# A recommendation tower rewritten: 11 instead of 9 tables by one-hot matmul, split tables kept in an HBM scratch

## The reference

```python
e = stack([tbl_f[ids[:, f]] for f in range(26)], axis=1)      # 2048 x 26 x 128, fp32
combined = concatenate([dense[:, None, :], e], axis=1)        # 27 features of 128 per sample
inter = einsum('bfd,bgd->bfg', combined, combined)            # 27 x 27 per sample
z = concatenate([dense, inter[:, iu, ju]], axis=1)            # 128 + 351 pairs above the diagonal
h = relu(concatenate([z, dense], axis=1) @ W_top1 + b_top1)   # 607 -> 512
h = relu(h @ W_top2 + b_top2)                                 # 512 -> 256
y = h @ W_top3                                                # 256 -> 1
```

## Time and profile before

| | |
|---|---|
| median of three runs | 431.82 us (426.78, 431.82, 437.46) |
| the profiled execution: its span, which is its time here | 432.4 us |
| prologue, to the first gram | 0 to 79 us |
| a block in the loop | 99 us |
| last gather issued | 392.3 us |
| data moved | 49.5 MB, 115 GB/s |

### The profile page before, as it was taken

The page is one execution under the profiler, slowest core; times in us unless marked ns, Lnnn a source line. Parts: engine busy times, 40 slices in busy tenths (PEclk is TensorE's granted clock), DMA queues, the critical chain, the costliest instruction groups (busy, mean ns, idle before and its releaser), DMA issues.

```text
span 432.4 us, 13310 instructions
## 1 busy us (share of the span) xinstructions
PE 330.4 (76%) x5360; PEld 266.8 (62%) x5360; DVE 239.1 (55%) x471; ACT 179.4 (41%) x363; POOL 308.9 (71%) x280
## 2 busy tenths in 40 slices
PE   0785719677699998286879999376969999867596
PEld 0563517466578876275668877264758887656475
DVE  2776625397569563266768664075666758023531
ACT  2144223720746546220546545420564546323442
POOL 6887878887778877777778878777777877772000
PEclk9899977888979999659969999666879999986699
DMA  5467853435435345426444543526354442221000
GB/s 155 153 177 191 239 167 109 128 92 151 115 110 149 118 122 117 133 52 167 119 130 114 158 116 106 141 55 169 77 172 100 142 123 71 55 57 28 5 0 0
DMA packets 24707, 49.51 MB, mean 115 GB/s; under 512 B 8010, under 2 KB 10586, under 8 KB 24653
## 3 DMA queue, kind: packets, MB, share of 16 engines
q1 hardware_dynamic: 15916, 30.83, 22.4%
q0 software_dynamic: 8704, 17.84, 17.5%
q10 hardware_dynamic: 32, 0.01, 0.0%
HBM read 48.65 MB, written 0.01 MB: 113 GB/s over the span
## 4 chain that ended last, share of the span: by engine, by line
PE 65%; issue 15%; DMA 10%; ACT 5%; DVE 3%; SPq 0%; ACTq 0%; DVEq 0%
PE mix_ps L454 12%; PE emb_ps L436 12%; PE emb_ps L438 11%; PE emb_ps L416 6%; DMA lookup_ids<-ids_looked_up 5%; DMA table<-table 5%; PE mlp_ps L485 4%; PE mlp_ps L488 4%; PE mlp_ps L486 4%; PE mlp_ps L436 3%; PE mlp_ps L438 3%; DVE one_hot L650 2%; ACT emb L535 2%; PE mlp_ps L498 2%; PE mlp_ps L501 2%
## 5 line engine op out<-in xcount | busy, mean ns | idle before, releaser
L396 POOL DMA_INDIRECT rows<-table,gather_ids x272 | 307.9, 1132 | 83.6 <-issue 81.7
L650 DVE TENSOR_SCALAR one_hot<-lookup_ids,row_number 125x512 fp32r<-125x512 int32 x288 | 124.8, 490 | 43.6 <-DMA lookup_ids<-ids_looked_up 17.6
L436 PE MATMUL emb_ps<-one_hot,table_h 125*128 125x512 f32 x224 | 94.2, 421 | 19.1 <-DVE table_l L640 18.7
L454 PE MATMUL mix_ps<-emb 128*26 128x26 f32 x4096 | 57.7, 202 | 54.3 <-issue 51.5
L438 PE MATMUL emb_ps<-one_hot,table_l 125*128 125x512 f32 x224 | 91.9, 410 | 0.0
L454 PEld LDWEIGHTS mix_ps<-emb 128*26 128x26 f32 x4096 | 49.5, 115 | 63.6 <-issue 61.7
L543 ACT ACTIVATE table_h<-table 125x1024 fp32r<-125x1024 f32 x36 | 38.0, 1060 | 88.9 <-DMA table<-table 52.4
L535 ACT ACTIVATE emb<-emb_ps 128x512 f32<-128x512 f32 (+1 forms) x80 | 46.9, 651 | 56.5 <-PE emb_ps L416 53.2
L663 DVE COPY gram<-mix_ps 128x416 f32<-128x416 f32 x32 | 27.8, 874 | 74.3 <-PE mix_ps L454 74.1
L436 PEld LDWEIGHTS emb_ps<-one_hot,table_h 125*128 125x128 f32 x224 | 44.6, 199 | 31.7 <-ACT emb L535 12.1
L549 ACT ACTIVATE emb<-emb_ps 128x512 f32<-128x512 f32 x28 | 34.0, 1215 | 50.2 <-PE emb_ps L438 50.1
(11 more groups left out here) (50 smaller groups left out, 278.4 us busy)
## 6 DMA issues: line engine op xcount, KB each, us to landing
table<-table SPq DMA_DIRECT2D x36, 500.0 KB
lookup_ids<-ids_looked_up SPq DMA_DIRECT2D x36, 256.0 KB, 5.4
rows<-table,gather_ids POOLq DMA_INDIRECT x272, 3.9
dense_rows<-dense SPq DMA_DIRECT2D x4, 256.0 KB, 4.1
gram<-w_pairs SPq DMA_DIRECT2D x2, 256.0 KB
gram<-w_dense SPq DMA_DIRECT2D x2, 256.0 KB
h_full<-w SPq DMA_DIRECT2D x1, 512.0 KB
gather_ids<-ids_gathered SPq DMA_DIRECT2D x16, 8.5 KB, 10.2
```

Of the source, the lines that this page charges most:

```text
L396: pool.indirect_dma_start(out=rows[:, t, g, :], out_offset=None, in_=tables[GATHERED[g]], in_offset=bass.IndirectOffsetOnAxis(ap=gather_id ...
L436: pe.matmul(bank[:, :], table_h[0:TROWS, i % 2, cols], hot, start=(c == 0), stop=False)
L454: last = pe.matmul(bank[32 * j:32 * j + SIDE, SIDE * q:SIDE * q + SIDE], emb[:, s, 1:FEATURES], emb[:, s, 0:SIDE], start=True, stop=True)
L650: dve.tensor_scalar(one_hot[0:TROWS, hot_slot(i, c), :], lookup_ids[0:TROWS, i % 2, :], row_number[0:TROWS, c:c + 1], None, ALU.is_equal) \
```

## The change

The kernel is rewritten. It computes the same thing with other numbers, layouts and orders.

- 11 tables are looked up, and 15 are gathered: 16 x 15 = 240 gathers. `rows` holds two tiles (`ROWS = 2`). The gathers of tile t wait, four by four, for the transposes of tile t-2.
- The tables are loaded and split once, in the prologue. Both parts (1 MB a table) are then written to an HBM tensor `scratch` (`spill`), and blocks 1 to 3 load both parts from there (`load`, else branch), 33 loads of 1 MB. Three buffers (`HL = 3`).
- Tables are padded to 1024 rows, the ids come as int16. ACT writes a second copy of the ids less one (`less`), so that DVE makes two one-hot matrices with one instruction of 1024 elements (`hots`, four per lookup).
- `emb` is laid out `[128, feature, sample]`: features are written contiguously, and a gram reads its 26 numbers with a step of 128 elements (512 B).
- Everything is unrolled. One list STEPS, sorted by times in units of blocks, sets the order on every engine. Gram halves (64 matmul records) alternate with lookup halves (8 matmuls) and with parts of the tower; the tower of a block runs during the next. Lookups of block b run from time b-1. In the prologue (time -1 to 0) stand the 11 lookups and the four transposes of tile 0 alone.
- The weights are issued by SP at time 0.06, behind the prologue; ACT and DVE wait for them at 0.06.
- The last block's tower is two units of two tiles (256 columns).
- The triangle is copied by ACT alone with 10 instructions for two tiles.

```diff
-LOOKUPS = 9
+LOOKUPS = 11
+    SPLIT_BLOCKS = 1
+    HL, RAW, LIDS, ROWS = 3, 3, 2, 2
+    UNITS = [(0, 4), (4, 4), (8, 4), (12, 2), (14, 2)]
+    def look_time(k, h):
+        b, i = divmod(k, LOOKUPS)
+        return b - 1 + (i + h / 2 + (0.3 if b > 0 else 0.0)) / LOOKUPS
+    for k in range(LOOKS):
+        at(look_time(k - 3, 1) if k >= 3 else -2.0 + k / 10, "load", k)
+        at(look_time(k - 2, 1) + 0.002 if k >= 2 else -1.9 + k / 10, "less", k)
+        if k < SPLIT_BLOCKS * LOOKUPS:
+            at(look_time(k - 1, 0) - 0.001 if k >= 1 else -1.5, "split", k)
+        if SPLIT_BLOCKS - 1 == k // LOOKUPS and SPLIT_BLOCKS < BLOCKS:
+            at(look_time(k, 0) - 0.002, "spill", k)
+        for h in range(2):
+            at(look_time(k - 1, h) + 0.001 if k >= 1 else -1.4 + h / 10, "hots", k, h)
+            at(look_time(k, h), "look", k, h)
+    for t in range(TILES):
+        at((t - 4) / PER_BLOCK + 0.01 if t >= 4 else -1.95 + t / 10, "drow", t)
+        for e in range(EMBEDS):
+            at((t + 0.02 + 0.06 * e) / PER_BLOCK if t > 0 else (-0.6, -0.5, -0.4, -0.3)[e], "embed", t, e)
+        for n in (2 * t, 2 * t + 1):
+            for h in range(2):
+                at((t + 0.4 + 0.3 * (n % 2) + 0.14 * h) / PER_BLOCK, "gram", n, h)
+        if t % 2 == 1:
+            at((t + 1.1) / PER_BLOCK, "pairs", t // 2)
+    for j in range(6):
+        at(0.06 + 0.12 * j, "weights", j)
...
+        def _(sp):
+            def load(k):
+                i, s = k % LOOKUPS, k % HL
+                if is_split(k):
+                    wait(sp, table_low, k - RAW + 1)
+                    sp.dma_start(raw[:, k % RAW, :],
+                                 tables[LOOKED_UP[i]].rearrange("(p c) d -> p (c d)", c=CHUNKS)) \
+                        .then_inc(raw_in[k % RAW], 16)
+                else:
+                    wait(sp, hot_used, QUADS * (k - HL + 1))
...
+                    sp.dma_start(table_hl[:, s, :, :].bitcast(fp32), scratch[i]).then_inc(hl_in[s], 16)
+                wait(sp, hot_ready, QUADS * (k - LIDS + 1))
...
+                sp.dma_start(lids[:, k % LIDS, 0, :],
+                             ids_looked_up[i:i + 1, col:col + BLOCK].to_broadcast([128, BLOCK])) \
...
+            def spill(k):
+                sp.wait_ge(table_low, k + 1)
+                sp.dma_start(scratch[k % LOOKUPS], table_hl[:, k % HL, :, :].bitcast(fp32)).then_inc(spilled[k % HL], 16)
...
+        def _(pool):
+            for t in range(TILES):
...
+                for e in range(EMBEDS):
+                    wait(pool, embeds_done, EMBEDS * (t - ROWS) + e + 1)
+                    for g in EMBED[e]:
+                        if g < NG:
+                            pool.indirect_dma_start(
+                                out=rows[:, t % ROWS, g, :], out_offset=None, in_=tables[GATHERED[g]],
...
+        def _(pe):
+            def look(k, h):
...
+                    if is_split(k):
+                        pe.wait_ge(table_low, k + 1)
                     else:
+                        pe.wait_ge(hl_in[k % HL], 16 * reloads(k))
+                for p in (2 * h, 2 * h + 1):
+                    pe.wait_ge(hot_ready, QUADS * k + p + 1)
+                    for c in (2 * p, 2 * p + 1):
...
-                                         emb[:, s, 1:FEATURES], emb[:, s, 0:SIDE], start=True, stop=True)
+                                         emb[:, f + 1:f + FEATURES, s], emb[:, f:f + SIDE, s], start=True, stop=True)
...
+        def _(act):
+            def less(k):
+                act.activation(lids[:, k % LIDS, 1, :], lids[:, k % LIDS, 0, :], ACT.Copy, bias=-1.0) \
+                    .then_inc(less_one, 1)
+            def split(k):
+                act.wait_ge(raw_in[k % RAW], 16 * (k // RAW + 1))
+                wait(act, hot_used, QUADS * (k - HL + 1))
+                if spills(k - HL) > 0:
+                    act.wait_ge(spilled[k % HL], 16 * spills(k - HL))
+                act.activation(table_hl[:, k % HL, 0, :], raw[:, k % RAW, :], ACT.Copy).then_inc(table_high, 1)
...
+        def _(dve):
+            def hots(k, h):
+                if h == 0:
+                    dve.wait_ge(less_one, k + 1)
+                for p in (2 * h, 2 * h + 1):
+                    wait(dve, hot_used, QUADS * (k - 1) + p + 1)
+                    dve.tensor_scalar(hot[:, p, :, :], lids[:, k % LIDS, :, :],
+                                      row_number[:, 2 * p:2 * p + 1], None, ALU.is_equal).then_inc(hot_ready, 1)
```

More of the change, by code:

```diff
@@ L105, in dlrm_tower @@
-    BODY = [("gram", 0), ("gram", 1), ("gram", 2), *tile2, ("gram", 3), ("gram", 4),
-            *early, *tile3[:-1], ("dense",), ("gram", 5, 0), tile3[-1], ("gram", 5, 1),
-            ("split", EARLY + 1), ("pair", 0), ("gram", 6), ("gram", 7)]
-    EMB_USES = [s for s in TAIL + BODY if s[0] == "embed" or (s in halves and s[2] == 1)]
-    MIX_USES = [("gram", n) for n in range(GRAMS)] + [("z", 0), ("z", 1), ("z", 2)] + [("none",)]
-    MLP_USES = [("place", i) for i in range(EARLY)] + [("layer1", n) for n in range(N1)] + \
-        [("layer2", n) for n in range(N2)] + [("layer3",), ("none",)]
@@ new lines, in dlrm_tower @@
+    STEPS = [step for _, _, step in sorted(timed)]
+    emb_bank_of, emb_before = {}, {}
+    last_step = [None] * 3
+    through = [-3, -2, -1]
+    for now, s in enumerate(STEPS):
+        if s[0] == "embed" or (s[0] == "look" and s[2] == 0):
+            i = through.index(min(through))
+            assert through[i] < now
+            emb_bank_of[s], emb_before[s] = i, last_step[i]
+            last_step[i] = s if s[0] == "embed" else ("look", s[1], 1)
+            through[i] = STEPS.index(last_step[i])
@@ new lines, in features, with places @@
+        def features(tile):
+            return WIDE * (PLACES - 1 - PLACE[tile])
+        def places(b, f):
+            tiles = range(b * PER_BLOCK, (b + 1) * PER_BLOCK)
+            even = all(PLACE[t] == PLACE[t - 1] + 1 for t in tiles[1:])
+            for run in ([tiles] if even else [tiles[:-1], tiles[-1:]]):
+                first = (features(run[0]) + f) * TILE
+                pitch = (PLACES * WIDE - 1) * TILE
+                yield (slice((run[0] - tiles[0]) * TILE, (run[-1] + 1 - tiles[0]) * TILE),
+                       bass.AP(emb, first, [[pitch, 128], [-WIDE * TILE, len(run)], [1, TILE]]))
@@ L378, in _ @@
+            sp.dma_start(gather_ids[:, 0, :], ids_gathered[:, 0, :]).then_inc(first_ids_in, 16)
+            run({"load": load, "spill": spill, "drow": drow, "weights": weights})
         @block.gpsimd
@@ L442, in grams @@
[L442 to L451 removed]
+                    wait_emb_bank(pe, use)
```

883 lines of the change are left out of this document (402 added, 481 removed).

## The result

| | before | changed |
|---|---|---|
| median of four runs | 430.8 us (426.8 to 437.5) | **459.8 us** (456.4 to 462.2) |
| ratio | | **1.068**, 95% interval 1.057 to 1.079 |
| profiled execution: span, time | 432.4, 431.8 | 454.5, 456.4 |
| first gram of tiles 0, 4, 8, 12 | 78.8, 176.7, 276.0, 373.6 | 76.8, 175.8, 273.7, 369.5 |

The forecast was 419. The last line, read from the first L454 and L434 records of each block, already tells most of it: three blocks of 99.0, 97.9 and 95.8 us, where 85 were forecast, and before they took 97.9, 99.3 and 97.6. (The first of them has 14 us of waiting for the weights in it, but no tower yet; the forecast had given it one.) The issue pauses are gone, and a block still lasts as long. The last block takes 85.0 us to the end, 58.8 before: it holds the tower of block 2 besides its own. So against the kernel before the time is lost there.

A forecast was written before the change was run, and what follows sets the result against it. POOL's gathers were taken to bound the kernel before (391 us), PE nearly as tight. Prologue 89 + weights 6 + first tile 21 + gathers 269 + end 34 = 419 us, against 422 by PE; range 384 to 448.

The forecast's parts named there:

- sum by POOL: Whole time along POOL: prologue 89, weights 6, first tile 21, last 195 gathers 269, end 34, together 419 us.
- first tile: After prologue and weights, a quarter of the first block passes before POOL goes on gathering: 21 us.
- end: From the last gather to the finish, mostly the last tower with 256-column matmuls: 34 us (28 to 40).
- part 2: PE's block: wide matmuls 57.0 us, 1024 gram records at 16 ns 16.4, transposes 9.9; 85 us with layer 3 and clock.
- sum by PE: Whole time along PE: 89 + 6 + three blocks of 85, then 30 gathers 38 and end 34, together 422 us.
- Part 1: POOL's gathers, 240 instead of 272: after its standstill 165 at 1.40 us and 30 at 1.25, together 269 us.
- Rival (c): PE's gram reads with a 512 B step cost 28 ns a record, not 16, +12 us a block: 461 us; chance 0.13.
- rival (d): PE's granted clock stays at 0.88 in the blocks, +14 us each: 464 us, or 440 at 0.95; chance 0.08.
- Part 3: Prologue of 11 lookups with spills to HBM: 12 + 11 x 7 = 89 us to the first gram (75 to 112).
- rival (b): Prologue takes the gain: HBM writes share DMA engines badly, 9 us a lookup, weights 12: 447 us, or 432; chance 0.18.
- Part 4: Weights, 1.75 MB issued at 0.06 behind spills and reloads, hold up the first block for 6 us (0 to 13).
- POOL sets a floor of 391 us: Kernel before: 272 gathers at 1.438 us each bound it, 39 us of PE work follow, and PE is nearly as tight.

The follow-up runs named there:

- sample_major_3: Changed kernel with emb laid out [sample, slot], so grams read neighbours and ACT writes with a step; first kind of chip: 413.2 us, ratio 0.961 to the kernel before.
- after_quiet_pool: Changed kernel, grams still stepped, with the gathers of tiles 2 to 15 left out; second kind of chip: 469.2 us.
- before_quiet_pool: Kernel before with the gathers of blocks 1 to 3 left out; first kind of chip: 427.0 us (420.1 and 433.9).
- sample_major_2: The same kernel as sample_major_3, run on the second kind of chip: 622.7 us, ratio 0.888 to the kernel before.

## Why the prediction was wrong, step by step

The sum by POOL, with the same places read in the changed kernel and in the repaired one, both on chips of the first kind:

| term | forecast | changed | sample_major_3 |
|---|---|---|---|
| first gram | 89 | 76.8 | 76.9 |
| weights, PE idle | 6 | 14.0 | 13.9 |
| first tile, to POOL's restart | 21 | 20.0 | 17.6 |
| 195 gathers | 269 | 308.5 | 266.1 |
| end | 34 | 35.2 | 34.7 |
| sum | 419 | 454.5 | 409.2 |

**The step that failed is the gram record of part 2**, "1024 gram records at 16 ns", in a sum that gave the new layout the price of the old one's reads. It takes 23.7 ns from start to start, against 10.7 with neighbours in the same kernel. With all that passes until PE's next matmul it comes to 30.8 ns in the changed kernel and 18.7 in sample_major_3, so the term is 31.5 and 19.1 us a block, for the 16.4 of the forecast. The expected gain of a block was 98 - 85 = 13 us, from the pauses and the clock; the stepped reads took 13 to 15 us back, so the block stayed where it was. The sum by PE shows it: 422, less 12 for the prologue, and 8 for the weights, 24 for the three blocks (85.0, 97.9 and 95.8 for 3 x 85) and 13 for the last one (85.0 for 38 + 34) make 455. Counted with all their pauses (nothing else on PE between them, distances up to 5 us) gram records stand 24.7 ns apart before and 23.7 after: the pauses were exchanged for the step. With neighbours they stand 12.2 apart and the blocks of sample_major_3 take 85.3 and 84.9 us between the first transposes of tiles 4, 8 and 12 (161.8, 247.1, 332.0): the 85 of the forecast. Only block 0 had been mis-thought, in the sum by PE: without a tower, and apart from the weights, it takes 85.0 us in the changed kernel (99.0 - 14.0) and 79.2 in the repaired one.

**Part 1's pace was wrong by the same cause.** (418.0 - 110.75) / 194 = 1.584 us a gather, 1.40 or 1.38 forecast; in sample_major_3 (373.33 - 108.44) / 194 = 1.365. The share of slow gathers was put down to DVE's work, which was right, but that work was taken to be as long as before; the stepped reads lengthen it. Of the last 195 gathers 26 take over 2 us in the changed kernel and none in sample_major_3, in the mean they take 1277 and 1029 ns. Here rows of POOL in the changed kernel, with the restart and the last gather:

```profile
62.99 1.61 POOL L382 DMA_INDIRECT rows<-table,gather_ids  x1 [0.30 <-issue]
110.75 1.44 POOL L382 DMA_INDIRECT rows<-table,gather_ids  x1 [46.15 <-PE emb_ps L418]
418.01 0.95 POOL L382 DMA_INDIRECT rows<-table,gather_ids  x1 [0.30 <-issue]
```

Was it PE or POOL then? PE was enough: after_quiet_pool's blocks take 98.8, 97.7 and 95.8 us without the gathers, for 99.0, 97.9 and 95.8 with them. Its span is 471.3 with a first gram at 94.2, 17.4 later than in the changed kernel; without those it is 453.9, for 454.5. But POOL didn't simply follow: after its restart it waited for PE 1.5 us in all, and its gathers filled the rest at 1.28 us each and 0.30 between. The two were level again, both slowed by the same reads. What quick gathers would have given beside stepped reads on this kind of chip no run shows.

**Rival (c) was the case.** It named PE's L454 (L434 now), the step of 512 B and 461 us; 459.8 came. Its price of 28 ns was 16 ns times the factor of ACT's copy. Both ends were too high (10.7 and 23.7), but the difference of 12 was near the 13 measured, and this is what its sum uses. That the price of ACT's copy carries over to PE so well was luck, and so in part is the time: prologue and weights were 4 us off in all. The 23 ns from which it decides don't follow from its own terms either; 422 passes 440 from 16 + 18 / (3.25 x 1.024) = 21.4 ns on. The rule of the Trainium skill ("SBUF — State Buffer", Door 1), that accesses which reach a new 16-byte line each time pay, agrees with the one step that was run, 512 B: 10.6 ns for neighbours, 16 with one operand stepped and 23.7 with both. I gave it 0.13 because "16 ns hold at both clock levels". That reads the earlier trace rows wrongly: there the 16 ns stand at the lower level, and the 128 records in 1.28 us, 10 ns each, at the upper one. The stretches of the kernel before about the two (granted clock third from the end):

```profile
278.70:280.80 2.10, 2.04 (x127) 1.86 (x128) 0.35 (x1) 0.00 (x0) 1.49 (x3) 0.50 0.20 51
399.00:400.40 1.40, 1.28 (x128) 1.17 (x127) 1.40 (x2) 0.15 (x1) 0.00 (x0) 1.00 0.06 12
```

So the price of a near record at the upper level was on view. Nothing in the earlier trace rows told whether its pace was set by issue or by reads, and ACT's row was the only one of a stepped access to the same buffer.

**What was right.** The issue pauses are gone: the group L434 idles 2.1 us in all, against 51.5 of "issue" in the kernel before. The clock is 1.00 in the blocks, so not rival (d). The end is 35 for 34, the first tile 20 for 21. What took the issue pauses away isn't shown by itself. By the Trainium skill's rule on branches ("Runtime: NRT & Kernel Launch", Instruction fetch mechanics) it could be the missing jump, but the written-out last block of the kernel before had the pauses too, so the work between the gram halves is the likelier cause.

**Part 3 was pessimistic by 12 us.** The first gram came at 76.8. In their best stretch the DMA engines moved 384 to 390 GB/s (part 2 of the page, slices 3 to 5), well above the 275 reckoned for a full mixture. The big writes to HBM did not stand in the way of the loads: 1 MB lands in 7.0 us, half a MB of table in 7.5 (the page's last lines above). So rival (b) fell.

**Part 4 was 8 us short**, above its own range of 0 to 13. PE and ACT in the changed kernel:

```profile
98.80 0.79 PE L402 MATMUL emb_ps<-hot,table_hl 128*128 128x512 f32 x1 [13.98 <-DVE hot L619]
96.73 0.63 ACT L598 ACTIVATE w1h<-w_stage 128x512 fp32r<-128x512 f32 x1 [17.02 <-DMA b_sb<-b]
```

Parts 3 and 4 nearly cancel (-12 and +8).

**And what bounds the kernel before was read wrong.** "POOL sets a floor of 391 us" is right as arithmetic, but before_quiet_pool lacks that floor and still takes 420 to 434. PE with its issue pauses was the bound, and the gathers were worth 4 to 6 us a block. Both rows were there; I called the two level and let the sum follow POOL.

## The second kind of chip

There the kernel before takes 1.6 times as long. Gram records stop while POOL issues gathers. sample_major_2, rows of PE's matmuls and POOL in order of time, a gram without gathers and then one with them:

```profile
213.34 0.73 PE L434 MATMUL mix_ps<-emb 128*26 128x26 f32 x64
...
224.41 0.46 PE L434 MATMUL mix_ps<-emb 128*26 128x26 f32 x21
224.41 0.94 POOL L382 DMA_INDIRECT rows<-table,gather_ids  x1 [0.30 <-issue]
225.40 0.21 PE L434 MATMUL mix_ps<-emb 128*26 128x26 f32 x2 [0.53 <-issue]
225.66 0.95 POOL L382 DMA_INDIRECT rows<-table,gather_ids  x1 [0.30 <-issue]
226.13 0.18 PE L434 MATMUL mix_ps<-emb 128*26 128x26 f32 x1 [0.52 <-issue]
226.86 0.22 PE L434 MATMUL mix_ps<-emb 128*26 128x26 f32 x2 [0.55 <-issue]
...
228.98 0.33 PE L434 MATMUL mix_ps<-emb 128*26 128x26 f32 x4 [1.90 <-issue]
231.12 0.28 PE L434 MATMUL mix_ps<-emb 128*26 128x26 f32 x3 [1.81 <-issue]
```

64 records in 0.73 us alone; beside gathers 21 and then one to four at a time, 0.7 us or a multiple of it apart. Over the whole kernel records with nothing else on PE between them (distances up to 5 us) stand 230 ns apart in the mean while POOL is in a run of gathers and 16 otherwise, on the first kind of chip (sample_major_3) 12.6 and 9.4. The 512-column matmuls are not held: beside gathers too they start every 0.23 us (from 222.46 on). With POOL silent the same kernel takes 414 us: it is the gathers that cost the 210 us. POOL in turn waits for PE's transposes (247.1 us in sample_major_2). That the changed kernel is 8% faster there may come from its 32 fewer gathers; this was not tried by itself. What differs between the chips, and why records of 26 columns are held and wide ones not, stays open.

## To carry to other kernels

Price a layout from the reader's side as well as the writer's: the edit that made 1 copy instruction cheaper made 256 records of small matmuls a tile dearer. When a trace shows one instruction slowed by stepping through a buffer, price the next engine that will step through it by that factor before calling the risk small. Before a price is said to hold at both clock levels, read the granted clock beside each row that it rests on. And where two engines look level, ask which would still give the time if the other were gone.

## Not expected of the hardware

- A 26-column fp32 record costs 10.6 ns reading neighbours, 16 with one operand 512 B apart, 24 to 28 with both. No other step was run.
- With both stepped, PE's reads slow ACT and DVE beside them: ACT's 512-column copy 2352 ns for 688, DVE's one-hot pair 2099 for 747 (after_quiet_pool). With one stepped hardly anything is left of it. Gathers of over 2 us, 26 in the changed kernel, lie where DVE works beside a stepped gram.
- On four chips small matmuls are held in steps of 0.7 us while POOL issues indirect DMAs: 414 us without and 623 with them.
- Open: whether earlier weights and a third tile of `rows` would give anything on the first kind of chip. On the second the earlier weights took the 14 us of idle away and made the prologue 11 to 12 us longer; beside the near reads the two edits gave 3 to 13 us.
